# Three reorderings and a score row by way of DRAM in a four-layer graph network kernel

## The reference

```python
h = jnp.maximum(_layernorm(x, axis=-1), 0.0)
x = x + _L0_gnn_ref(h, adj, ...)   # adj.T softmax, two matmuls, two batch norms over all graphs
h = jnp.maximum(_layernorm(x, axis=-1), 0.0)
x = x + _L1_gnn_ref(h, adj, W, a)  # e = leaky_relu(s_i + t_j), masked softmax, times Wh
h = jnp.maximum(_layernorm(x, axis=-1), 0.0)
x = x + _L2_gnn_ref(h, adj, ...)   # e = leaky_relu(sum_d h_i h_j a_d), masked softmax, times h
h = jnp.maximum(_layernorm(x, axis=-1), 0.0)
x = x + _L3_gnn_ref(h, adj, W, a)  # as layer 1 with another W, a, then elu
```

## Time and profile before

| what | value |
|---|---|
| median of 3 runs | 1505.93 us (1505.83 to 1507.24) |
| the profiled execution | 1506.49 us, span from first to last instruction 1504.7 us |
| PE / PEld / DVE / ACT / POOL busy | 91% / 82% / 78% / 54% / 26% of the span |
| granted TensorE clock, mean | 0.964 |

### The profile page before, as it was taken

The page is one execution under the profiler, slowest core; times in us unless marked ns, Lnnn a source line. Parts: engine busy times, 40 slices in busy tenths (PEclk is TensorE's granted clock), DMA queues, the critical chain, the costliest instruction groups (busy, mean ns, idle before and its releaser), DMA issues.

```text
span 1504.7 us, 33033 instructions
## 1 busy us (share of the span) xinstructions
PE 1375.7 (91%) x12642; PEld 1238.7 (82%) x12642; DVE 1177.1 (78%) x3400; ACT 818.6 (54%) x1843; POOL 384.2 (26%) x337
## 2 busy tenths in 40 slices
PE   5899998899946888999999999999999999999886
PEld 5899997555536778999999999989999889999785
DVE  5788885788746668888888898888988889887565
ACT  4788885122243564565746656556565565654621
POOL 6343430000010304314133141331423314223020
PEclk9999998899968989999999999999999999999998
DMA  9999993566612213132331432314323134132111
GB/s 206 224 226 231 223 217 130 183 241 239 208 39 76 71 41 94 50 106 83 94 93 50 113 100 71 95 51 109 106 64 99 52 104 113 44 86 56 30 43 44
DMA packets 111840, 169.36 MB, mean 113 GB/s; under 512 B 9808, under 2 KB 61760, under 8 KB 109632
## 3 DMA queue, kind: packets, MB, share of 16 engines
q1 hardware_dynamic: 87264, 125.20, 28.9%
q0 software_dynamic: 19584, 33.56, 12.3%
q10 hardware_dynamic: 4832, 8.45, 1.5%
HBM read 158.74 MB, written 42.00 MB: 133 GB/s over the span
## 4 chain that ended last, share of the span: by engine, by line
PE 48%; DVE 11%; DVEq 4%; ACT 3%; POOL 2%; issue 2%; ACTq 0%
PE ps L1703 31%; PE ps L1662 3%; PE ps L1685 2%; PE ps L1716 2%; PE ps L1630 2%; DVE wts_C L1010 2%; PE ps L1674 2%; PE ps L1676 2%; PE ps L1675 2%; POOL wts_B L923 1%; DVEq L1033 1%; DVE xC L1087 1%; DVE st_B L945 1%; DVE xB L1040 1%; PE ps L1639 1%
## 5 line engine op out<-in xcount | busy, mean ns | idle before, releaser
L1703 PE MATMUL ps<-hV,wts_B 128*128 128x129 f32 x2048 | 252.4, 279 | 13.0 <-POOL wts_B L923 5.2
L923 POOL TENSOR_TENSOR wts_B<-wts_B,off 128x1024 f32<-128x1024 f32 (+7 forms) x128 | 177.8, 1413 | 323.0 <-PE ps L1685 323.0
L1703 PEld LDWEIGHTS ps<-hV,wts_B 128*128 128x128 f32 x2048 | 241.3, 194 | 17.4 <-POOL wts_B L923 7.3
L1703 PE MATMUL ps<-hP_A,wts_A 128*128 128x129 f32 x1920 | 230.9, 275 | 1.1 <-ACT xB L1429 0.7
L1703 PEld LDWEIGHTS ps<-hP_A,wts_A 128*128 128x128 f32 x1920 | 221.5, 191 | 3.8 <-DVE hP_C L994 2.9
L1703 PE MATMUL ps<-hP_C,wts_C 128*128 128x129 f32 x1920 | 220.1, 274 | 0.0
L1703 PEld LDWEIGHTS ps<-hP_C,wts_C 128*128 128x128 f32 x1920 | 217.4, 191 | 0.5
L1010 DVE SCALAR_TENSOR_TENSOR wts_A<-row_A,least_A,ring_A 128x1024 f32<-128x1024 f32 x128 | 161.0, 1274 | 11.4 <-ACT row_A L1384 7.9
L1010 DVE SCALAR_TENSOR_TENSOR wts_C<-row_C,least_C,ring_C 128x1024 f32<-128x1024 f32 x120 | 166.7, 1401 | 0.0
L316 ACT ACTIVATE maskT<-ps 128x1024 fp8e4<-128x1024 bf16 x128 | 131.2, 1025 | 45.4 <-PE ps L360 33.0
L372 PE MATMUL ps<-x,adj_b 128*128 128x129 f16 x896 | 121.3, 224 | 20.9 <-DVE x L237 13.9
(11 more groups left out here) (243 smaller groups left out, 2713.7 us busy)
## 6 DMA issues: line engine op xcount, KB each, us to landing
adj_b<-in_adj POOLq DMA_DIRECT2D x120, 256.0 KB, 10.4
maskT_scratch<-maskT SPq DMA_DIRECT2D x16, 1024.0 KB, 6.8
ring_A<-maskT_scratch SPq DMA_DIRECT2D x64, 256.0 KB, 3.1
off<-maskT_scratch SPq DMA_DIRECT2D x32, 512.0 KB, 6.6
ring_C<-maskT_scratch SPq DMA_DIRECT2D x64, 256.0 KB, 3.4
xa<-in_x SPq DMA_DIRECT2D x16, 512.0 KB, 16.3
whT_b<-whT_scratch SPq DMA_DIRECT2D x16, 512.0 KB, 4.8
pTf_scratch<-pT_b SPq DMA_DIRECT2D x16, 512.0 KB, 2.9
```

Of the source, the lines that this page charges most:

```text
L923: pool.tensor_tensor(w, w, off_fp8[:, k, k * P:N], ALU.mult).then_inc(S["B", "up"], 1)
L1703: last = nc.tensor.matmul(Q_SLOTS[c // 2 % 2][:, c % 2, 0:PW], wts[y][:, j, c * P:c * P + P], src[:, j, :], start=(j == 0), stop=(j == T - 1))
```

## The change

1. Stage 1: in DVE's `graph`, `shifts`, the two `normed`, `high` and `low` stand one block earlier: at c = 2, 2 and 3, 4, 5 instead of 3, 3 and 4, 5, 6.
2. Stage 2: `later_weights_dve` stands behind the second `graph`, and `later_weights_pe` behind the second `rows` and the first `product`.
3. Stage 3: layer 1 of graphs 3 to 15 takes the way by DRAM for its score row (`VIA["A"]`). On PE one `row_once` behind step 4 of B takes the place of 8 transposes; on ACT `store_row` stands in front of the first `normed("B")`, and both `row_power` go; on SP's queue `load_row("A")` stands behind `load_x`. On DVE `columns("A")` (what the peak is made from) goes in front of `weights("C", ., 4)`, `weights("A", ., 0)` to `2` go behind the statistics of C, and `elu_negative` takes the place where they were.

```diff
@@ stage 1, DVE
-                            if more and c == 3:
+                            if more and c == 2:
                                 shifts(b + 1)
-                            if more and 3 <= c < 5:
-                                normed(b + 1, c - 3)
+                            if more and 2 <= c < 4:
+                                normed(b + 1, c - 2)
+                            if more and c == 4:
+                                high(b + 1)
                             if more and c == 5:
-                                high(b + 1)
-                            if more and c == 6:
                                 low(b + 1)
@@ stage 2, DVE
                     graph(0, 0, True)
+                    graph(1, 1, True)
                     later_weights_dve(dve)
-                    graph(1, 1, True)
@@ stage 2, PE
                     rows(0, 0, 0, True)
-                    later_weights_pe(pe)
                     rows(1, 1, 0, False)
                     product(0, 0, True)
+                    later_weights_pe(pe)
@@ stage 3
-            VIA = {"A": range(0), "C": range(0, B - 2)}
+            VIA = {"A": range(3, B), "C": range(0, B - 2)}
@@ SP
                             load_x(i + 2)
+                        if i + 1 in VIA["A"]:
+                            load_row("A", i + 1)
@@ DVE
-                        if post and GW:
+                        if post and GW and i + 1 not in VIA["A"]:
                             elu_negative(i - 3)
...
+                        if nextA and i != 0:
+                            columns("A", i + 1)
                         if CA:
                             weights("C", i - 2, 4)
                         if nextA and i != 0:
-                            columns("A", i + 1)
                             exponents("A", i + 1)
...
                             weights("C", i - 2, 7)
-                        if nextA and i != 1:
+                        if post and GW and i + 1 in VIA["A"]:
+                            elu_negative(i - 3)
+                        if nextA and i != 1 and i + 1 not in VIA["A"]:
                             weights("A", i + 1, 0)
...
                             moments("C")
+                        if i + 1 in VIA["A"]:
+                            weights("A", i + 1, 0)
+                            lowest("A", i + 1)
+                            weights("A", i + 1, 1)
+                            weights("A", i + 1, 2)
@@ ACT
                             scaled("B", i - 1, 0)
+                        if i + 1 in VIA["A"]:
+                            store_row("A", i + 1)
                         if AA:
                             normed("B", i, newB, 0)
...
-                        if nextA and i != 0:
+                        if nextA and i != 0 and i + 1 not in VIA["A"]:
                             row_power("A", i + 1, 0)
@@ PE
-                                if c in (4, 5):
+                                if c in (4, 5) and i + 1 not in VIA["A"]:
                                     rows("A", i + 1, free_p, c - 4)
+                                if c == 4 and i + 1 in VIA["A"]:
+                                    row_once("A", i + 1, free_p)
```

More of the change, by code:

```diff
@@ L1301, in run @@
                                 weights("A", 2, j)
-                        if nextA and i + 1 not in EARLY:
+                        if nextA and i + 1 not in EARLY and i + 1 not in VIA["A"]:
                             weights("A", i + 1, 2)
```

## The result

The changed kernel takes 1530.98 us (median of 4 runs, 1528.37 to 1532.67) beside 1506.59 us for the kernel before in the same session: a ratio of 1.0159 with a 95% interval of 1.0145 to 1.0172. It is slower, as forecast, by 24.4 us where 20 were forecast. The profiled execution took 1528.37 us, its span is 1526.6 us: 21.9 us above the span of before. Two of the four runs lie some 4 us above it; what these 4 us are, no trace here shows.

A forecast was written before the change was run, and what follows sets the result against it. PE's work was taken to set stage 3's turn, with DVE, ACT and PE holding each other in stage 1. Terms +18.2 - 3.7 + 5.9 = +20.4 us gave 1526 us for the median; range 1505 to 1538.

The forecast's parts named there:

- Stage 1, +18.2: Stage 1: the move delays ACT's divisors, a graph takes 15.54 us instead of 14.16; thirteen graphs give +18.2 us.
- the count of block 6 is now made behind `low`: Stage 1, DVE: this count ends at 137.85, so ACT's division of block 6 begins 1.82 us later.
- the groups from block 3 on: Stage 1, DVE: the groups from c = 3 on come later by one place each; no separate size given.
- The rule of the Trainium skill: Stage 1: up to -13.9 us instead of +18.2 (chance 0.05); carried through all three edits, 1473 us (chance 0.06).
- Stage 2, -3.7: Stage 2, PE: without L533's wait in front, the second rows begins earlier and the third at 281.77 instead of 285.44.
- the trace has 285.44 - 274.21 = 11.23: Stage 2, PE: time from second to third rows, taken from the old trace, with 0.45 added for L533.
- Stage 3, +5.9: Stage 3: PE is late by 0 to 0.5 us a turn, taken as +0.45; thirteen turns give +5.9 us.
- The PE side: Stage 3, PE: without the peak's wait and with fewer transposes, step 6 of B could begin 1.21 us earlier.
- ACT's queue: Stage 3, ACT: store_row queued ahead of normed and scaled holds step 6 until 841.30, giving back all of the 1.21 us.
- The DVE side: Stage 3, DVE: later first sum of B and added elu_negative delay C's third shares and scaled; turn_h("C") 0 to 0.5 late.
- `weights("A")` 0 to 2 only change places within this stretch: Stage 3, DVE: moving them was charged no time up to the shares of C's third pair.
- The `elu_negative` that was charged with it: Stage 3, DVE: elu_negative adds 1.3 us up to the shares of C's third pair.

The follow-up runs named there:

- graph_one_block_later: On the kernel before, shifts to low in stage 1 moved one block later (c = 4, 4 and 5, 6, 7); 1544.94 us, ratio 1.0263, +39.5 us.
- low_one_block_earlier: On the kernel before, only low in stage 1 moved one block earlier, shifts, normed and high staying; 1517.22 us, ratio 1.0078, +11.8 us.
- later_weights_alone: On the kernel before, only the stage 2 edit: later weights behind the second rows and first product; 1500.64 us, ratio 0.9970, -5.2 us.
- store_behind_scaled: Only the stage 3 edit, with ACT's store_row behind scaled of B's second pair; 1495.79 us, ratio 0.9936 against the kernel before, -10.1 us.
- store_and_weights_mended: Stage 2 and 3 edits, store_row behind scaled("B"), layer 1's weights 0 to 2 in their old place; 1503.18 us, ratio 0.9984 against the kernel before.

## Why the prediction was right

The direction and the signs of the three terms were right. The terms missed by +2.1, -2.2 and +1.5 us in the traces, so that their sum, 20.4 beside 21.9, is nearer than its parts: that is partly luck.

**Stage 1, +18.2; measured 20.3 in the changed kernel, +18.8 alone.** Right: `shifts` can't start earlier, x is no sooner behind it, ACT is late by 1.8 us at block 6, and a graph takes 15.5 us. The working of the cause was right only in part. The step "the count of block 6 is now made behind `low`" was taken for the whole delay; the groups from block 3 on, which the forecast named in half a sentence, carry most of it, and block 6's adds to an ACT that is late already. The sum also had no term for PE's wait of 1.37 us for `rest` of block 2, which DVE's order alone makes. That both ways lead to 1.8 us is luck. Part of the 2.1 us more is before's shorter mean: from the 4th to the 16th `shifts` a graph takes 15.53 us instead of 13.95, where the one graph shown took 14.16; 12 x 1.58 = 19.0 of the 20.1 us at the last `shifts`.

The rule of the Trainium skill weighed in the prediction ("Perfetto Trace Analysis", Optimization Strategy: find the gaps of the busiest engine and make what they wait for start sooner) held from graph_one_block_later to the kernel before, where x did set the pace and making it sooner paid, and failed from there to low_one_block_earlier, where PE's gap at L372 was closed and 11.8 us were lost. The kernel before sits between the two.

**Stage 2, -3.7; measured -5.9, alone -5.2.** The mechanism is right; the size hangs on PE's clock, which the forecast did not weigh. The step "the trace has 285.44 - 274.21 = 11.23" carried the durations of before over, and the second `rows` among them had run at half clock. Where it still does, in the trace of later_weights_alone, the term comes out (-3.6). In the changed kernel's trace, of the 2.2 us more, 1.2 are the second `rows` (2.36 us up to `product`, with a new wait of 0.34 for its row, instead of 3.56), 0.7 the `product` behind it (7.67 us before, whose first matmuls were slow too; 6.9 now) and 0.6 the first `rows` (6.00 us up to the second instead of 6.57); L533 gives 0.25 back, since DVE's `w_fine` was late by 0.30. The 0.6 are not the edit's, which stands behind the first `rows`: in the nine traces with the old order its first 2.2 us were granted anything from 0.50 (before) to 1.00.

**Stage 3, +5.9; measured 7.4, alone +8.2.** The PE side and ACT's queue were right to a few hundredths, and store_behind_scaled shows the queue by itself: without it 1.4 us of each turn come off. The DVE side had the right end (0.45 us a turn forecast, 0.55 measured) from a wrong cause: counted from a peak without its wait, as the forecast did, the transposes for layer 3 are 0.75 late, and 0.2 come back up to the next peak. The step that failed is "`weights("A")` 0 to 2 only change places within this stretch": their place is what costs the 0.57 us between the two transposes. The `elu_negative` that was charged with it costs nothing, and gains 0.1. From the first to the last of the 13 peaks, twelve turns, the changed kernel takes 749.76 us instead of 741.47: 8.3 more, of which 12 x 0.55 = 6.6, and most of the rest in a single turn of 64.50 us (62.01 before). In it a piece of DVE's work that is done once (L1061 to L1069, 1.7 us) stands ahead of C's last shares, and PE then waits 0.92 us, up to 0.1 behind the end of ACT's `scaled` that had waited 1.57 for these shares; what follows in that turn is open. The last of the 13 turns loses 1.2 up to its transposes for layer 3; the stretches ahead of the peaks and behind these transposes gain 0.5 and 1.6.

## What to carry to other kernels

A wait of the busiest engine says which result is late, not that moving it forward helps: first look at what the producer itself waits for, and at everything that the move puts behind it in the same in-order queue, above all at what the busiest engine needs from there. Before a removed wait is priced from durations of a trace, look at the clock at which these had run. When a piece of work on PE is replaced by a small one on ACT and a DMA, the place of that small one in ACT's order decides the sign: here 1.4 us a turn between in front of and behind one `scaled`. And work that "only changes places" on a full engine is to be followed to the next result that somebody waits for; splitting a run of four into one and three was worth more than the whole change had cost there.

## What was not expected of the hardware

PE's granted clock after standing still does not follow from the length of the wait alone in these traces. Behind the 7.29 us ahead of L533 the second `rows` was granted 0.50 (1.2 GHz) in all nine traces with the old order, and took 3.55 us up to the next instruction. Behind 3.73 us it was granted 1.00 (2.4 GHz) and took 2.02 in the changed kernel, 0.50 and 3.54 in later_weights_alone, and 0.65, 0.66 and 0.75 (means over the stretch) in the three other traces with the new order. Behind only 2.4 to 2.8 us of waiting in stage 1 of graph_one_block_later, the 3.19 us that followed were granted 0.50 to 0.54 in eleven graphs in a row, and 1.00 in the graph ahead of them. So a wait can cost 1.5 us more than its own length, on work that stands behind it, and the same wait can cost nothing more.

The row lands 3.3 to 4.2 us behind its issue in store_and_weights_mended (median 3.6). DVE waited for it between 0.17 and 1.98 us in 10 of 13 turns, and not at all in the others. That is a wider range than the landing's own, so the instants of issue and of need move too.
